# A recommender kernel on one core: the remainder of layer 0 moved from VectorE to GpSimd, its gathers rescheduled, and repeated products at the start

## What is computed

```python
e = jnp.stack([tbl_0[ids[:, 0]], ..., tbl_38[ids[:, 38]]], axis=1)      # 2048 x 39 x 16
xk = x0 = e
for idx, (W, b) in enumerate([(w0, b0), (w1, b1), (w2, b2)]):           # 128 outputs each
    z = relu(jnp.einsum('bhd,bkd,hks->bsd', x0, xk, W) + b[None, :, None])
    if idx != 2:
        xk = z[:, :64, :]; direct.append(z[:, 64:, :])
    else:
        direct.append(z)
z = jnp.sum(jnp.concatenate(direct, axis=1), axis=-1)                   # 2048 x 256
h = relu(concat([z, dense_ctx]) @ W_top1 + b_top1)
h = relu(h @ W_top2 + b_top2)
y = h @ W_top3
```

## Time and profile before

| | |
|---|---|
| median of 3 runs | 2597.91 us (2596.68 to 2600.87) |
| profiled execution | 2598.07 us, span 2596.2 us |
| mean granted clock of TensorE | 0.984 |
| PE busy | 2443.5 us, 94% of the span |
| DVE busy | 2169.6 us, 84% |
| GpSimd (POOL) busy | 1875.1 us, 72% |
| ACT busy | 1661.3 us, 64% |
| moved by DMA | 352.58 MB |

### The profile page before, as it was taken

The page is one execution under the profiler, slowest core; times in us unless marked ns, Lnnn a source line. Parts: engine busy times, 40 slices in busy tenths (PEclk is TensorE's granted clock), DMA queues, the critical chain, the costliest instruction groups (busy, mean ns, idle before and its releaser), DMA issues.

```text
span 2596.2 us, 32413 instructions
## 1 busy us (share of the span) xinstructions
PE 2443.5 (94%) x8654; PEld 1591.3 (61%) x8654; DVE 2169.6 (84%) x1872; ACT 1661.3 (64%) x2120; POOL 1875.1 (72%) x1270
## 2 busy tenths in 40 slices
PE   0899999999999999999999999999999999999989
PEld 0466666666656666666666666666666666666655
DVE  1588889889878888988988898898888888888880
ACT  1566666666666666766666676666666666666653
POOL 6578778777867777777787777778777777765450
PEclk6899999999999999999999999999999999999999
DMA  2677667667757766766776676677667666756730
GB/s 71 139 149 155 126 138 166 134 131 151 154 110 152 154 130 132 166 137 132 148 158 129 132 164 140 127 150 155 131 131 166 141 131 145 160 129 129 159 80 0
DMA packets 214715, 352.58 MB, mean 136 GB/s; under 512 B 34382, under 2 KB 47566, under 8 KB 214588
## 3 DMA queue, kind: packets, MB, share of 16 engines
q1 hardware_dynamic: 194717, 347.07, 61.6%
q0 software_dynamic: 19968, 5.15, 2.2%
HBM read 346.97 MB, written 5.12 MB: 136 GB/s over the span
## 4 chain that ended last, share of the span: by engine, by line
POOL 30%; issue 27%; PE 16%; DVE 9%; DMA 7%; ACT 7%; SPq 3%; POOLq 0%; ACTq 0%; DVEq 0%; another core or an unknown queue 0%
POOL emb L374 13%; POOL Pl L380 13%; DMA xb<-x_dram 7%; ACT Ph L514 5%; PE ps L807 5%; PE ps L797 4%; DVE P L692 3%; DVE ps L692 3%; PE ps L817 3%; POOL dir L404 3%; SPq L311 3%; DVE Pl L697 3%; PE ps L926 1%; PE ps L918 1%; POOL emb L385 1%
## 5 line engine op out<-in xcount | busy, mean ns | idle before, releaser
L380 POOL TENSOR_TENSOR Pl<-P,Ph 128x1024 fp32r<-128x1024 f32 x448 | 1072.3, 2397 | 479.1 <-ACT Ph L514 469.4
L692 DVE TENSOR_TENSOR P<-xb,ps 128x1024 f32<-128x1024 f32 x768 | 926.8, 1214 | 81.1 <-DMA xb<-x_dram 72.9
L807 PE MATMUL ps<-Ph,wh 128*128 128x512 f32 x1920 | 870.1, 459 | 8.1 <-ACT Ph L514 8.0
L697 DVE TENSOR_TENSOR Pl<-ps,Ph 128x1024 fp32r<-128x1024 f32 x512 | 626.1, 1223 | 178.9 <-ACT Ph L514 168.7
L374 POOL DMA_INDIRECT emb<-tbl_in,idx x624 | 601.0, 963 | 166.3 <-issue 145.3
L807 PE MATMUL ps<-Ph,wl 128*128 128x512 f32 x1792 | 707.4, 395 | 0.0
L514 ACT ACTIVATE Ph<-ps 128x1024 fp32r<-128x1024 f32 x512 | 523.3, 1022 | 285.3 <-DVE ps L692 217.3
L817 PE MATMUL ps<-Pl,wh 128*128 128x512 f32 x1920 | 689.7, 445 | 11.4 <-POOL Pl L380 11.3
L514 ACT ACTIVATE Ph<-P 128x1024 fp32r<-128x1024 f32 x448 | 474.6, 1059 | 325.3 <-DVE P L692 303.8
L692 DVE TENSOR_TENSOR ps<-xb,ps 128x1024 f32<-128x1024 f32 x512 | 628.2, 1227 | 28.1 <-DMA xb<-x_dram 10.2
L797 PE MATMUL ps<-P,wp 128*128 128x512 f32 x1280 | 603.7, 594 | 4.1 <-DVE P L692 4.1
(11 more groups left out here) (64 smaller groups left out, 826.7 us busy)
## 6 DMA issues: line engine op xcount, KB each, us to landing
xb<-x_dram SPq DMA_DIRECT2D x1280, 256.0 KB, 8.5
emb<-tbl_in,idx POOLq DMA_INDIRECT x624
x_dram<-rows_sb SPq DMA_DIRECT2D x64, 78.0 KB
xb<-w_in SPq DMA_DIRECT2D x15, 128.0 KB
xb<-wt_in SPq DMA_DIRECT2D x2, 512.0 KB, 8.6
xb<-dense_in SPq DMA_DIRECT2D x1, 768.0 KB, 5.9
wp<-w_in SPq DMA_DIRECT2D x5, 128.0 KB
xb<-w0a_in SPq DMA_DIRECT2D x1, 448.0 KB
```

The source lines that it names most:

```text
L380: pool.tensor_tensor(Pl[:, h_slot(ref, c, k)], P[:, p_slot(ref, c, k)], Ph[:, h_slot(ref, c, k)], ALU.subtract).then_inc(low_pool, 1)
L692: dve.tensor_tensor(p, xb[:, x], xk.unsqueeze(1).broadcast_to([128, 2, N]), ALU.mult)\
L697: dve.tensor_tensor(Pl[:, h_slot(ref, c, k)], p_ps, Ph[:, h_slot(ref, c, k)], ALU.subtract)\
L807: pe.matmul(z_of(c, k), w[:, q, j, :], Ph[:, h_slot(ref, c, k), j, :], start=k in (L1B, L2) and i + j == 0, stop=False)
```

## The change

1. ACT's second square of the remainder goes to SBUF: `rest_sq`, 12 partitions of a tile `rows` that also holds rows_sb. It squares rows 0 to 11, so the low part now lies in the first of the three parts. ACT's square frees the PSUM bank.
2. The subtraction goes from DVE to GpSimd, at step 16 (`REST_AT`), for all chunks but the first two, which stay on DVE.
3. The gathers stand in a table `GATHERS`, one at a step in most places: 9, 10, 11 and 9 in the four chunks where there were 9, 9, 12 and 9. The ids of the tile after next are copied at step 18 of the second chunk, ahead of two of its gathers, and no longer at the third chunk's start.
4. ACT's `full_emb` moves from step 15 to 17.
5. At the start PE multiplies 36 times the same weights (fp32, 128x512) into a bank that is overwritten later, after its first small matmuls. The first `low_emb` goes from GpSimd to DVE. The sums of the first chunk go to several banks (`early_ps`), and in the first two chunks the remainder comes first among the sums.

```diff
-REST_AT = 1
+REST_AT = 16
-HIGH_AT, FULL_AT, LOW_AT = 15, 15, 17
+HIGH_AT, FULL_AT, LOW_AT = 15, 17, 17
-GATHER_AT = [k for k in range(STEPS) if KIND[k] != "G"]
+NEXT_IDS_AT = (1, 18)
+GATHERS = [[1, 2, 3, 5, 9, 14, 16, 17, 18], [1, 2, 3, 5, 6, 8, 9, 10, 18, 18],
+           [1, 2, 3, 5, 6, 9, 10, 12, 14, 16, 17], [1, 2, 3, 5, 6, 8, 9, 10, 17]]
...
+        early_ps = (ps[:, 6, :], ps[:, 7, :], aux_ps, ps[:, 7, :], aux_ps, ps[:, 7, :], aux_ps)
...
+            def rest_low(T, chunk):
+                pool.wait_ge(rest_high, T * CPT + chunk + 1)
+                pool.wait_ge(rest_square, T * CPT + chunk + 1)
+                pool.tensor_tensor(sqx[LOWS, :], rest_sq, sqx[LOWS, :], ALU.subtract).then_inc(rest_ready, 1)
...
+                        if k == REST_AT and not (last and c >= 2):
+                            rest_low(T, c + 2)
+                        if (c, k) == NEXT_IDS_AT and todo[2]:
+                            next_ids(T + 2)
...
+            def rest_squares(T, chunk, number, bank=aux_ps):
+                act.wait_ge(aux_ready, T * PER["aux"] + number + 1)
+                act.activation(sqx[:, :], bank[0:REST0], ACT.Square).then_inc(rest_high, 1)
+                act.activation(rest_sq, bank[LOWS], ACT.Square).then_inc(rest_square, 1)
...
-            def rest_low(T, chunk):
-                dve.wait_ge(rest_square, T * CPT + chunk + 1)
-                dve.tensor_tensor(sqx[LAST_LO, :], aux_ps[LAST_LO], sqx[LAST_LO, :], ALU.subtract).then_inc(aux_read, 1)
...
+            for i in range(WARM):
+                pe.matmul(z1_ps[:, 0], wp[:, 0, 0, :], wp[:, 0:2].rearrange("p q j m -> p (q j m)"), start=True, stop=True)
...
+                            if t < FULL0:
+                                pe.wait_ge(aux_read, aux + 2 + t)
+                            else:
+                                pe.wait_ge(rest_ready, T * CPT + c + 3)
+                            contract0(t, c % 2, opens, t == T0 - 1)
```

More of the change, by code:

```diff
@@ L414, in _ @@
                 gather(f)
-            low_emb(0)
             def next_ids(T):
@@ L431, in tile @@
             def tile(T, ref, fields, first=False, last=False):
+                todo = [list(f) for f in fields]
                 for c in range(CPT):
-                    if c == 2 and fields[c]:
-                        next_ids(T + 2)
-                    todo = list(fields[c])
-                    slots = [k for k in GATHER_AT if c != 1 or k < FOLD0A_AT - 4]
                     for k in range(STEPS):
@@ L440, in tile @@
                             low(T, ref, c, k)
-                        if k in slots:
-                            n = -(-len(todo) // len(slots[slots.index(k):]))
-                            for f in todo[:n]:
-                                gather(f)
-                            todo = todo[n:]
+                        if k == REST_AT and not (last and c >= 2):
+                            rest_low(T, c + 2)
+                        if (c, k) == NEXT_IDS_AT and todo[2]:
+                            next_ids(T + 2)
+                        part = min(c, 1) if (c, k) < NEXT_IDS_AT else 2
+                        n = GATHERS[c].count(k) * (1 + (first and c == 0))
+                        for f in todo[part][:n]:
+                            gather(f)
+                        todo[part] = todo[part][n:]
                         if c == 0 and not first and k in FOLD1_AT:
@@ L463, in tile @@
                             low_emb(T + 1)
-            cuts = (0, 12, 21, 30, NF)
-            third, fourth, first, second = (range(a, b) for a, b in zip(cuts, cuts[1:]))
-            tile(0, 0, (range(early, 30), range(30, NF), third, fourth), first=True)
+            late, soon = len(GATHERS[0]), len([k for k in GATHERS[1] if (1, k) < NEXT_IDS_AT])
+            cut = NF - late - soon
+            assert sum(map(len, GATHERS)) == NF
+            start, middle, rest = range(0, cut), range(cut, cut + late), range(cut + late, NF)
+            tile(0, 0, (range(early, cut + late), rest, start), first=True)
             with pool.Fori(1, TILES - 2) as T:
-                tile(T, 1, (first, second, third, fourth))
-            tile(TILES - 2, TILES - 2, (first, second, (), ()))
-            tile(TILES - 1, TILES - 1, ((), (), (), ()), last=True)
+                tile(T, 1, (middle, rest, start))
+            tile(TILES - 2, TILES - 2, (middle, rest, ()))
+            tile(TILES - 1, TILES - 1, ((), (), ()), last=True)
             pool.wait_ge(z2_read, chunks)
@@ L537, in _ @@
                 copy_x(0, AUX * g)
-                for t in range(T0):
-                    square(0, AUX * g + 1 + t, t)
-                    s = t - (T0 - PRE - 1)
+                if g:
+                    rest_squares(0, 1, AUX + 1)
+                for t in range(FULL0):
+                    square(0, AUX * g + 2 + t, t, aux_ps if g else early_ps[t + 1])
+                    if t == 0 and not g:
+                        rest_squares(0, 0, 1, early_ps[0])
+                    s = t - (FULL0 - PRE)
                     if g and 0 <= s < PRE and KIND[L1B + s] != "P":
@@ L738, in tile @@
                         waiting = (T, ref, c, k) if KIND[k] == "V" else None
-                        if k == REST_AT and not end and not (first and c == 0):
-                            rest_low(T, c + 1)
                         if end and k == L2 + 5:
@@ L851, in _ @@
             late = None
-            for g in range(2):
-                number = AUX * g
-                if g:
-                    pe.wait_ge(aux_read, number)
-                transposes(g)
-                for t in range(T0):
-                    pe.wait_ge(aux_read, number + 1 + t)
-                    sums(t)
-                    if t:
-                        contract0(t - 1, g)
-                    if g and t >= T0 - PRE:
-                        late = contract(0, 0, -1, L1B + t - (T0 - PRE), late)
-                pe.wait_ge(aux_read, AUX * (g + 1))
-                contract0(T0 - 1, g)
+            transposes(0)
+            pe.wait_ge(aux_read, 1)
+            for i, t in enumerate((FULL0, 0, 1)):
+                sums(t, early_ps[i])
+            for t in range(FULL0):
+                pe.wait_ge(aux_read, 2 + t)
+                contract0(t, 0, t == 0, False)
+                if t + 2 < FULL0:
+                    sums(t + 2, early_ps[t + 3])
+            pe.wait_ge(rest_ready, 1)
+            contract0(FULL0, 0, False, True)
+            transposes(1)
+            order = (FULL0, *range(FULL0))
+            for i, t in enumerate(order):
+                if i == 1:
+                    pe.wait_ge(rest_square, 2)
+                else:
+                    pe.wait_ge(aux_read, READS + max(i, 1))
+                sums(t)
+                if i == 1:
+                    pe.wait_ge(rest_ready, 2)
+                if i:
+                    contract0(order[i - 1], 1, i == 1, False)
+                if i >= T0 - PRE:
+                    late = contract(0, 0, -1, L1B + i - (T0 - PRE), late)
+            pe.wait_ge(aux_read, 2 * READS)
+            contract0(FULL0 - 1, 1, False, True)
             assert not late
```

66 lines of the change are left out of this document (39 added, 27 removed).

## The result

The changed kernel takes 2619.67 us (median of 4 runs, 2617.76 to 2622.2); the kernel before, on the same chip, 2597.3 (4 runs, 2593.55 to 2600.87). The ratio is 1.009, 95% interval 1.0078 to 1.0103: slower by 22 us, where 26 us faster was predicted. It is outside the predicted range. The profiled execution of the changed kernel has a span of 2620.4 us against 2596.2, 24.2 more.

A forecast was written before the change was run, and what follows sets the result against it. PE was taken as the bound, with one steady hole waiting for DVE's subtraction, beside the load burst and GpSimd. Chunk ends gave 22 us and the start 4, together 26: 2572 us, 8-in-10 range 2535 to 2596.

The forecast's parts named there:

- The hole: PE's idle time before the remainder's matmul, waiting for DVE's subtraction: 55.0 us, 71 us with its full cost; to disappear.
- Second chunk's end: GpSimd's low part of step 19 comes 2.4 us late; this chunk end loses 1.0 us instead of gaining 1.4.
- a rival with a chance of 0.10 and a price of 1.7: PE's clock falls at each late low part, losing 1.7 us each, 24 us over 14: 2596 us; chance 0.10.
- First, third and fourth chunks' ends: Gains per tile: 0.68 us in the first and 0.53 in the third, limited by the load burst; about 1.0 in the fourth.
- The start: Before layer 1's first product: transposes 1.2 us earlier, then 2.8 more until ACT reads z0; 4 us gained, from 2 to 7.
- The repeated products: 36 products in PE's idle time before the transposes end before 60 us; clock expected down again by the transposes, gain nothing.
- The rival of a gather held up: A gather held directly before step 19's low part delays PE; at 4 us a tile it adds 56: 2628 us; chance 0.10.
- the two rivals on the fast side: GpSimd's low part at second chunks' ends not late, 2538 us, chance 0.15; the load burst not holding PE, 2523, chance 0.08.
- that the loads do not hold PE: The load burst does not limit PE, so the whole 71 us and the start are gained: 2523 us; chance 0.08.
- that GpSimd is not late: The second chunk's end gains 1.4 us instead of losing 1.0, 34 us more: 2538 us; chance 0.15.

The follow-up runs named there:

- Experiment 3: Changed kernel plus twelve extra products on TensorE in the wait ahead of step 19's low part of each second chunk: 2601.87 us.
- experiments 1 and 2: Changed kernel with the second chunk's two late gathers moved to the third chunk: ids copy moved too, 2564.87 us; ids copy left, 2566.25 us.
- experiment 7: Kernel with reordered loads, old ids copy and 46 repeats, given gather tables placing gathers 113, 226, 339, 452, 565 at steps 6 to 10: 2542.03 us; second table 2555.59 us.
- Experiment 6: Loads for the next chunk's steps 0 to 5 issued first: on the changed kernel with old gathers 2540.68 us, on the changed kernel 2607.32, on the kernel before 2588.59.
- the first table of experiment 7: Kernel with reordered loads, old ids copy and 46 repeats, with gathers 113, 226, 339, 452, 565 put at steps 6 to 10: 2542.03 us.

## Why the prediction was wrong

**The hole: right.** It is gone, and the subtraction on GpSimd takes 1274 ns where 1.3 was taken. Twelve rows cost GpSimd what 128 do (L418 in the changed kernel, 128x512, has a mean of 1316 ns). DVE had needed 689 ns for the same rows, so GpSimd is slower by a factor of 1.85. The Trainium skill (GPSIMD Engine Reference, 4.1 Engine selection) has about two for elementwise work with two inputs, by which 1.38 us would be the estimate; the trace agrees roughly.

**Second chunk's end: the step that failed.** The prediction had the low part of step 19 2.4 us late and the chunk losing 1.0 a tile; it lost 3.3. The chain was the right one: from the end of ACT's second square to the end of the low part it had 9.4 us, and the trace shows 9.6. What it did not add is, first, that ACT's full_emb, now at step 17, ends at 1253.23 and holds the squares back: measured from step 7, the second square ends at 17.8 us in second chunks, where it was 17.5 before and is 17.3 in the other chunks. With a gap of 0.23 of GpSimd ahead of the ids copy, PE could have begun the third low matmul at 1260.81 and began it at 1263.85, 3.0 late, 0.6 more than forecast. The prediction said that the squares "end where they did". Second, the clock: 1.5 us more in 12 tiles. It was a rival with a chance of 0.10 and a price of 1.7, put aside since 2.1 us of idle time was expected where 2.68 had been seen to bring it down. With 2.49 to 2.94 us it fell in 12 of 14. The Trainium skill (TensorE: Matmul & The Clock Gate, Part 1) also has the half clock behind idle time; here two stalls of 2.93 and 2.96 us were spared, so the length of a stall alone did not decide. Experiment 3 shows that this part is real and separate, experiments 1 and 2 that the whole goes with two gathers. In the two spared chunks the loss is 1.8 a tile, so 0.8 of the 2.3 that were not forecast are the longer stall and 1.5 the clock. In sum, the 15 periods from second chunks went from 567.9 to 611.9 us, +44.0. Only the one of them without gathers is not late: its period is 36.5 where it was 38.0, a gain of 1.4, as forecast.

**First, third and fourth chunks' ends: the mechanism right, the size half.** The prediction capped the gain by the loads at 0.68 and 0.53 in the first and third and gave 1.0 to the fourth; measured are 0.48, 0.24 and 0.29. The margins had been read as PE's distance behind ACT's rounding in single chunks, with the loads' times taken as fixed. The fourth chunk's end was given 1.0 with no row for it, and was capped like the others. Over all tiles the three return 17.5 us (8.0, 5.3 and 4.2 from the traces' sums) where 2.2 x 15 = 33 were in the forecast; the 8.0 hold two single things that cancel: the period of chunk 16 fell by 5.5, since a pause of GpSimd (experiment 7) met it elsewhere, and that of the very first chunk grew by 5.2, as below. Experiment 6 shows that the loads are the cap: reordered, all periods go to 36.5 with the old gathers. With those of the change the first chunk stays at 37.10, since its low part of step 19 is late, by 0.26 us of waiting where the prediction had 0.4: near it, and as it said not the first limit there.

**The start: right where it was worked out, worth nothing where it counts.** The transposes came at 62.26 and z0 was read at 75.13, as forecast. But of the 3.8 us only 1.5 were left at PE's wait at 102.07 (103.60 in the earlier trace rows); where the rest went was not followed. Then the gathers that stand ahead of the low part of step 4 made PE wait 2.35 us for it at 114.27 (1.49 before), and the clock fell behind that stall and took the 1.5. Where four gathers stand there in place of six (the first table of experiment 7), that wait is gone and step 7 comes at 113.6 instead of 115.8. And the doubled gathers of the first chunk, six between the subtraction and step 19's low part, made a stall that the prediction did not look for:

```profile
146.90 1.22 PE L845 MATMUL ps<-Pl,wh 128*128 128x512 f32 x2 [3.94 <-POOL Pl L389]
```

That period was 43.3 instead of 38.1, 5.2 us lost; it is part of the first chunks' sum above. With the old gathers it is 37.8.

**The repeated products: right** that the clock is down again by the transposes.

**The rival of a gather held up** had a real mechanism, but not that place: it strikes five gathers of 624, and was in the kernel before too. Of the two rivals on the fast side, experiment 6 refutes that the loads do not hold PE, and the stall of 2.88 us that GpSimd is not late.

The pieces of the trace: +44.0 from second chunks, -17.5 from the others, the start 0, and -2.2 from the last tile's second chunk and all behind the last period. That is +24.3 against 24.2 of the spans. Between the forecast of -26 and this lie 50 us: 31 in the second chunks (+44 for a forecast of 14 lost and 1.4 gained), 16 in the other chunks, 4 at the start.

## What to carry to other kernels

When work moves to an engine in front of something that the bottleneck waits for, add up everything that engine does between its last slack and that delivery, in every variant of the loop body (the first tile with its doubled counts too), and also what the change has moved on the engine that feeds it. A stall of the bottleneck that is forecast near one seen to bring its clock down (2.1 and 2.68 us here) has to be priced with the clock. And before a hole is counted as gain, see where the next limit stands in each chunk: here 1.2 us of hole returned 0.3 to 0.7 in three of four chunks, even with the old gathers, until the loads were put in the order of their use, a change of one line.

## What the runs showed of the hardware

- GpSimd pauses behind every 113th gather of 128 rows, 3.0 to 3.3 us where few transfers run and up to 9.0 us in a burst of loads, at the same numbers in all fourteen traces. What is behind the number was not tried, nor was the burst's part in the length. Other gathers that directly follow one another are mostly 1.25 to 1.3 us apart from start to start.
- In the changed kernel's second chunks, stalls of PE of 2.49 to 2.94 us were followed by the lower clock level for 3.4 us in 12 tiles, at a price of 1.5 us; two stalls of 2.93 and 2.96 us were not. Stalls of 1.23 and 1.45 us (experiment 7, in nearly every tile) never were: the periods there are 36.6 plus the stall and 0.3, and the clock's record has no fall in those chunks. Filler matmuls of which nothing is read kept the clock up in all second chunks of experiment 3.
- A GpSimd subtraction on 12 partitions takes as long as an addition on 128 (1274 and 1316 ns for 512 columns), while DVE's took 689.
